# Experts: quarters of the first product of block b+1 and of the second product of block b in turn

## The reference, cut to what matters

```python
def _L0_ffn_ref(x, Wr, br, ln_g, ln_b, W1, b1, W2, b2):
    ...
    xn = (xt - mu) * jax.lax.rsqrt(var + LN_EPS)
    xe = xn[None, :, :] * ln_g[:, None, :] + ln_b[:, None, :]
    h = jax.nn.gelu(jnp.einsum('end,edh->enh', xe, W1) + b1[:, None, :], approximate=False)
    y = jnp.einsum('enh,ehd->end', h, W2) + b2[:, None, :]
    y_tok = jnp.transpose(y, (1, 0, 2))
    sel = jnp.take_along_axis(y_tok, top_idx[:, :, None], axis=1)
    out = (weights[:, :, None] * sel).sum(axis=1)
```

## Time and profile before

| | us |
|---|---|
| median of 3 timed runs | 3797.17 |
| lowest and highest of them | 3793.64, 3798.28 |
| span of the profiled execution, first to last instruction | 4365.6 |
| the experts stage in the profile | about 1370 to 2287 |

### The profile page before, as it was taken

One profiled execution on the slowest core, in us unless ns is written; L12 is line 12 of the kernel. 1 busy time (PEld: TensorE's weight loads), 2 busy tenths in 40 slices (PEclk: granted clock), 3 DMA queues, 4 the chain that ended last, 5 costly groups with the idle time before them and its releaser, 6 DMA issues. The chain is left out here.

```text
span 4365.6 us, 47498 instructions
## 1 busy us (share of the span) xinstructions
PE 3253.1 (75%) x15077; PEld 2484.5 (57%) x15077; DVE 1790.8 (41%) x5335; ACT 1496.2 (34%) x2892; POOL 2531.6 (58%) x2604
## 2 busy tenths in 40 slices
PE   1455565555446989988886798987989868999868
PEld 1344444444335777776764576655666645666547
DVE  4355565534353111111117333343333435676664
ACT  3233333323323112121115244443444434555520
POOL 6666666666643656565546666665666656666620
PEclk6677777777767999999988899988999979999978
DMA  6343334334312545554437454554544534555452
GB/s 194 111 122 109 117 115 118 116 108 120 101 40 98 176 157 179 172 185 156 157 124 269 124 146 136 149 159 116 144 138 142 166 107 143 150 153 152 135 175 103
DMA packets 396972, 609.34 MB, mean 140 GB/s; under 512 B 81648, under 2 KB 295319, under 8 KB 395943
## 3 DMA queue, kind: packets, MB, share of 16 engines
q0 software_dynamic: 115808, 279.40, 22.6%
q1 hardware_dynamic: 274182, 317.02, 22.4%
q10 hardware_dynamic: 6720, 9.74, 0.7%
HBM read 509.58 MB, written 96.33 MB: 139 GB/s over the span
## 5 line engine op out<-in xcount | busy, mean ns | idle before, releaser
L2983 POOL DMA_INDIRECT rows_h<-table,step_src x1138 | 1105.8, 972 | 688.6 <-issue 342.5
L3025 PE MATMUL bank_g<-rows_hl,counts_h 128*128 128x512 f32 x3773 | 1049.8, 422 | 89.0 <-issue 45.4
L975 POOL DMA_INDIRECT rows_r<-table,step_src x782 | 749.6, 959 | 405.2 <-issue 214.1
L3025 PEld LDWEIGHTS bank_g<-rows_hl,counts_h 128*128 128x128 f32 x3773 | 721.3, 194 | 301.9 <-issue 101.0
L1000 PE MATMUL bank_r<-rows_r,hots_r 128*128 128x257 f32 x1564 | 473.4, 457 | 457.4 <-ACT rows_r L985 227.3
L1000 PEld LDWEIGHTS bank_r<-rows_r,hots_r 128*128 128x128 f32 x1564 | 340.1, 227 | 567.6 <-ACT rows_r L985 261.6
L3184 ACT ACTIVATE counts_h<-piece_h 128x896 fp32r<-128x896 uint8 x539 | 498.1, 945 | 458.8 <-PE bank_g L3025 223.3
L1901 POOL DMA_INDIRECT kept_A<-one_d,place_d x424 | 420.7, 992 | 127.4 <-issue 127.1
L2016 PE MATMUL pY_e<-w_e,h_e 128*128 128x256 f32 x1680 | 421.7, 410 | 76.7 <-ACT h_e L1982 54.4
L1011 DVE TENSOR_SCALAR hots_r<-lane,step_dst 128x128 f32<-128x128 f32 x782 | 210.3, 289 | 593.3 <-remote 365.2
L1982 ACT ACTIVATE h_e<-pH_e,prm_e 128x256 f32<-128x256 f32 (+1 forms) x456 | 179.6, 455 | 733.7 <-PE pH_e L2005 486.5
(11 more groups left out here) (397 smaller groups left out, 3864.9 us busy)
## 6 DMA issues: line engine op xcount, KB each, us to landing
w_e<-in_L_ffn_W SPq DMA_DIRECT2D x114, 1024.0 KB
piece_h<-kept_A SPq DMA_DIRECT2D x539, 112.0 KB
kept_A<-zero_r SPq DMA_DIRECT2D x189, 112.0 KB
rows_h<-table,step_src POOLq DMA_INDIRECT x1138
table<-ACC SPq DMA_DIRECT2D x51, 256.0 KB
kept_sw<-vec_g SPq DMA_DIRECT2D x49, 256.0 KB
rows_r<-table,step_src POOLq DMA_INDIRECT x782
b_e<-in_L_ffn_b SPq DMA_DIRECT2D x57, 128.0 KB
```

Of the source, the lines that this page charges most:

```text
L975: nc.gpsimd.indirect_dma_start(out=r["rows"][:, x, 0:D], out_offset=None, in_=r["table"][:, :], in_offset=bass.IndirectOffsetOnAxis(ap=c[" ...
L2983: nc.gpsimd.indirect_dma_start(out=d["rows"][:, x, :], out_offset=None, in_=tables[l - 1][:, :], in_offset=bass.IndirectOffsetOnAxis(ap=c[ ...
L3025: mm = pe.matmul(sums, d["counts"][:, n % CV, x % PC, :], both.both(t), start=(x == 0 and i >= RINGED[l]), stop=(x == NT - 1))
```

## The change: what it does

- TensorE makes the first product of block b+1 and the second product of block b in turn, a quarter of the one and then a quarter of the other. Before the loop it makes the first product of block 0 alone. One turn of the loop over b is called a pass below.
- The turn of tokens moves: `turn(b + 2)` is now the last thing of pass b. `turn(1)` stands ahead of the loop.
- All waits for scaled inputs, weights and adds stand together at the beginning of a pass.
- `h` has two buffers, and gelu of block b waits for the second product of block b-2.
- VectorE makes the inputs of b+2 ahead of the adds of b. One semaphore, `s_xe`, now counts both the copied parameters and the scaled inputs, so that it grows by two for each block.
- The weights' loads are cut in two, `load_first` (`w1`) and `load_second` (`w2`, `b2`), each with semaphores of its own. `w1` of block b is loaded when the first product of b-3 is done, `w2` and `b2` of block b-1 when the adds of b-4 are done.
- GpSimd gathers tokens for b+3, then scatters the results of b, then issues edges. Before, it issued edges, gathered for b+2, and then scattered.
- Two semaphores of the stage ahead are used again, and counts on them start from its last value (`since`).

```diff
         @block.sync
         def _(sp):
             for b in range(WEIGHTS, NBLK):
-                sp.wait_ge(s_mm2, b - WEIGHTS + 1)
-                load_expert(sp, ins, moe, m, b, s_y)
+                sp.wait_ge(s_mm1, (b - WEIGHTS + 1) * (HJ // 2))
+                load_first(sp, ins, moe, m, b)
+                if b > WEIGHTS:
+                    sp.wait_ge(s_y, halves_before(b - WEIGHTS))
+                    load_second(sp, ins, moe, m, b - 1)
+            sp.wait_ge(s_y, halves_before(NBLK - WEIGHTS))
+            load_second(sp, ins, moe, m, NBLK - 1)
...
-                v.tensor_copy(prm[:, q, :], moe["prm"][:, bass.ds(e, 1), :].rearrange("p o n -> p (o n)")).then_inc(s_prm, 1)
-                v.wait_ge(s_prm, b + 1)
-                v.wait_ge(s_T, b + 1)
+                v.tensor_copy(prm[:, q, :], moe["prm"][:, bass.ds(e, 1), :].rearrange("p o n -> p (o n)")).then_inc(s_xe, 1)
+                v.wait_ge(s_xe, 2 * b + 1)
+                v.wait_ge(s_T, since + b + 1)
...
             inputs(0)
+            inputs(1)
             for b in range(NBLK):
-                if b + 1 < NBLK:
-                    inputs(b + 1)
+                if b + 2 < NBLK:
+                    inputs(b + 2)
                 if b > 1:
                     v.wait_ge(s_st[b % 2], 16 * halves_before(b, 2))
-                v.wait_ge(s_mm2, b + 1)
+                v.wait_ge(s_mm2, since + b + 1)
...
         def _(act):
             for b in range(NBLK):
                 w = block_of(b)[2] * P
+                if b > 1:
+                    act.wait_ge(s_mm2, since + b - 1)
                 for j in range(HJ // 2):
                     act.wait_ge(s_mm1, b * (HJ // 2) + j + 1)
...
+            def first(b, j):
+                q, halves = b % W, block_of(b)[2]
+                if b > 0:
+                    pe.wait_ge(s_h, (b - 1) * (HJ // 2) + j + 1)
+                for n in range(2):
+                    o = (2 * j + n) * P
+                    for k in range(KD):
+                        mm = pe.matmul(pH[j][:, n * BR:n * BR + halves * P], w1[:, q, k, o:o + P], xe[:, b % 2, k, 0:halves * P],
+                                       start=(k == 0), stop=(k == KD - 1))
+                mm.then_inc(s_mm1, 1)
+
+            def second(b, j):
+                q, halves = b % W, block_of(b)[2]
+                pe.wait_ge(s_h, b * (HJ // 2) + j + 1)
+                for i in (2 * j, 2 * j + 1):
+                    for m in range(halves):
+                        mm = pe.matmul(pY[m][:, 0:D], h[:, b % 2, i, m * P:(m + 1) * P], w2[:, q, i, :],
+                                       start=(i == 0), stop=(i == HJ - 1))
+                if j == HJ // 2 - 1:
+                    mm.then_inc(s_mm2, 1)
+
             turn(0)
+            pe.wait_ge(s_xe, 2)
+            pe.wait_ge(s_w1[0], 16)
+            for j in range(HJ // 2):
+                first(0, j)
+            turn(1)
             for b in range(NBLK):
-                q, halves = b % W, block_of(b)[2]
-                pe.wait_ge(s_xe, b + 1)
-                pe.wait_ge(s_w[q], 48 * (b // W + 1))
-                for j in range(HJ // 2):
...
                 if b + 1 < NBLK:
-                    turn(b + 1)
+                    pe.wait_ge(s_xe, 2 * b + 4)
+                    pe.wait_ge(s_w1[(b + 1) % W], 16 * ((b + 1) // W + 1))
+                pe.wait_ge(s_w2[b % W], 32 * (b // W + 1))
                 if b > 0:
                     pe.wait_ge(s_y, halves_before(b))
-                for j in range(HJ):
...
+                for j in range(HJ // 2):
+                    if b + 1 < NBLK:
+                        first(b + 1, j)
+                    second(b, j)
+                if b + 2 < NBLK:
+                    turn(b + 2)
...
-            for b in range(4):
+            for b in range(3):
                 tokens(b)
-                if b > 1:
-                    results(b - 2)
...
-            for b in range(2, NBLK):
-                if b + 1 < NBLK:
+            for b in range(NBLK):
+                if b + 3 < NBLK:
+                    tokens(b + 3)
+                results(b)
+                if 2 <= b < NBLK - 1:
                     for n in range(*(late * (halves_before(x) - first) // (COLS - 1 - first) for x in (b, b + 1))):
                         edges(nc, g, dram, d, EARLY[2] + n)
-                if b + 2 < NBLK:
-                    tokens(b + 2)
-                results(b)
```

More of the change, by code:

```diff
@@ L1801, in invert @@
         away = sb("away_i", [P, 3, P], F32, ctx)
-        s_c, s_v, s_hot, s_mm, s_act = sem("i_const"), sem("i_v"), sem("i_hot"), sem("i_mm"), sem("i_act")
+        s_c, s_v, s_hot, s_mm, s_act = sem("i_const"), sem("i_v"), m["s_hot"], m["s_mm"], sem("i_act")
         AWAY = [n for n in range(2 * NT) if squared(n)]
@@ L1809, in _ @@
             for b in range(WEIGHTS):
-                load_expert(sp, ins, moe, m, b)
+                load_first(sp, ins, moe, m, b)
+                load_second(sp, ins, moe, m, b)
         @block.gpsimd
@@ L1924, in experts @@
     with ExitStack() as ctx:
-        w1, w2, b2, s_w = m["w1"], m["w2"], m["b2"], m["s_w"]
+        w1, w2, b2, s_w1, s_w2 = m["w1"], m["w2"], m["b2"], m["s_w1"], m["s_w2"]
         tok = sb("tok_e", [P, 2, 2, D], F32, ctx)
@@ L1928, in experts @@
         xe = sb("xe_e", [P, 2, KD, BR], F32, ctx)
-        h = sb("h_e", [P, HJ, BR], F32, ctx)
+        h = sb("h_e", [P, 2, HJ, BR], F32, ctx)
         y = sb("y_e", [P, 2, 2, D], F32, ctx)
@@ L1935, in experts @@
         s_st = [sem(f"e_store{q}") for q in range(2)]
-        s_prm, s_T, s_xe, s_mm1, s_h, s_mm2, s_y = (sem("e_prm"), sem("e_T"), sem("e_xe"), sem("e_mm1"), sem("e_h"),
-                                                    sem("e_mm2"), sem("e_y"))
+        s_xe, s_mm1, s_h, s_y = sem("e_xe"), sem("e_mm1"), sem("e_h"), sem("e_y")
+        s_T, s_mm2, since = m["s_hot"], m["s_mm"], 2 * NT
         block = ctx.enter_context(nc.Block())
@@ L1981, in _ @@
                         k = 2 * j + n
-                        a = act.activation(h[:, k, 0:w], pH[j][:, n * BR:n * BR + w], ACT.Gelu,
+                        a = act.activation(h[:, b % 2, k, 0:w], pH[j][:, n * BR:n * BR + w], ACT.Gelu,
                                            bias=prm[:, b % 2, 2 * KD + k:2 * KD + k + 1])
@@ L1990, in turn @@
                 pe.wait_ge(s_tok[q], 16 * (halves_before(b, 2) + n))
+                if b > 0:
+                    pe.wait_ge(s_xe, 2 * b)
                 for m in range(n):
@@ L1994, in turn @@
                 mm.then_inc(s_T, 1)
-            turn(0)
-            for b in range(NBLK):
-                q, halves = b % W, block_of(b)[2]
-                pe.wait_ge(s_xe, b + 1)
-                pe.wait_ge(s_w[q], 48 * (b // W + 1))
-                for j in range(HJ // 2):
[L2002 to L2007, removed]
+            def first(b, j):
+                q, halves = b % W, block_of(b)[2]
+                if b > 0:
+                    pe.wait_ge(s_h, (b - 1) * (HJ // 2) + j + 1)
[5 more added lines that the diff above has]
+                mm.then_inc(s_mm1, 1)
@@ L2018, in _ @@
-                mm.then_inc(s_mm2, 1)
+                for j in range(HJ // 2):
[4 more added lines that the diff above has]
+                    turn(b + 2)
         @block.gpsimd
@@ L2024, in tokens @@
                 if b > 1:
-                    g.wait_ge(s_T, b - 1)
+                    g.wait_ge(s_T, since + b - 1)
                 for m in range(n):
@@ L2161, in mixture @@
         m = dict(w1=sb("w1_e", [P, WEIGHTS, KD, HID], F32, ctx), w2=sb("w2_e", [P, WEIGHTS, HJ, D], F32, ctx),
-                 b2=sb("b2_e", [P, WEIGHTS, D], F32, ctx), s_w=[sem(f"e_w{q}") for q in range(WEIGHTS)])
+                 b2=sb("b2_e", [P, WEIGHTS, D], F32, ctx), s_w1=[sem(f"e_w1{q}") for q in range(WEIGHTS)], s_w2=[sem(f"e_w2{q}") for q in range(WEIGHTS)], s_hot=sem("i_hot"), s_mm=sem("i_mm"))
         invert(nc, ins, dram, c, moe, d, m, sb, pb, sem)
@@ L2167, with expert_at, load_first, load_second @@
 WEIGHTS = 3
-def load_expert(sp, ins, moe, m, b, s_y=None):
-    q, i = b % WEIGHTS, block_of(b)[0]
-    e = sp.value_load(moe["expert"][0:1, i:i + 1], min_val=0, max_val=NE - 1)
+def expert_at(sp, moe, b):
+    i = block_of(b)[0]
+    return sp.value_load(moe["expert"][0:1, i:i + 1], min_val=0, max_val=NE - 1)
+def load_first(sp, ins, moe, m, b):
+    q, e = b % WEIGHTS, expert_at(sp, moe, b)
     w1_d = ins["L0_ffn_W1"].rearrange("e (k p) h -> p e k h", p=P)
+    sp.dma_start(m["w1"][:, q, :, :], w1_d[:, bass.ds(e, 1), :, :].rearrange("p o k h -> p (o k) h")).then_inc(m["s_w1"][q], 16)
+def load_second(sp, ins, moe, m, b):
+    q, e = b % WEIGHTS, expert_at(sp, moe, b)
     w2_d = ins["L0_ffn_W2"].rearrange("e (j p) d -> p e j d", p=P)
[L2175 to L2179, removed]
+    sp.dma_start(m["w2"][:, q, :, :], w2_d[:, bass.ds(e, 1), :, :].rearrange("p o j d -> p (o j) d")).then_inc(m["s_w2"][q], 16)
```

(1 more changed line is left out.)

## The result

| | before | changed |
|---|---|---|
| median, us | 3796.12 (4 runs, 3793.64 to 3798.28) | 3944.82 (4 runs, 3944.41 to 3945.12) |
| ratio, 95% interval | | 1.0396 [1.0381, 1.0411] |
| profiled span, us | 4365.6, and 3789.8 in a second profile (e1) | 3942.3 |

The changed kernel is 148.7 us slower; forecast were 151, with a range of 108 to 218. Its profiled span lies within 3 us of its timed runs, so this trace can be read as it stands.

A forecast was written before the change was run, and what follows sets the result against it. TensorE was taken to bound the experts stage, without waits in undisturbed blocks. Stops with start and end, 118 us, plus clock falls, 33, gave 151: from 3797 to 3948 us, range 3905 to 4015 (forecast's own 3925 to 3985).

The forecast's parts named there:

- 55 stops: Between passes, turn, VectorE's scalings and adds leave TensorE idle 1.92 us, 2.2 in all per full pass; 116 us.
- falls of the clock: TensorE's clock halves after half of the 38 full stops, 1.74 us each: 33 us, bounds 0 and 96.
- start, end, the rest of quarters in turn: Scalings of block 1 at the start, 1.4 us, and adds of block 55 at the end, about 1.1 us.
- late gathers of before, gone in the changed kernel: Token waits, 29.0 us in the first profile, taken as mostly the profile's own; gathers costed at nothing.
- The disturbed stretches: 16 stretches of the experts stage losing about 159 us to gelu and token waits, taken as mostly the profile's own.
- the other section: Skill page's "HAM oscillation" section: long idle gaps cool the clock, so these stops would cost nothing more (3915).
- the line that the profiled span would grow from 4365.6: The profiled span would grow by the same 151 us as the timed median.
- Edits costed at nothing: Gathers, cut weight loads, extra register load, doubled h, reused semaphores and parameter copy: no time on TensorE's path.
- The stop without the clock: Rival: TensorE keeps full clock through all stops, 3797 + 118 = 3915 us; chance 0.14.
- Faster: Rival: the lost 159 us are real in timed runs and the new order removes them all: 3756 us; chance 0.06.

The follow-up runs named there:

- e1: The kernel before, with no edit, profiled a second time: 3791.85 us, profiled span 3789.8 us.
- e10: Changed kernel plus 5 identity matmuls with unread results behind each turn of a pass, to keep TensorE busy: 3908.40 us, ratio 1.0302.
- e8: Changed kernel with turn in mid-pass, adds waited for behind the first quarter, and edges issued ahead of the scatter: 3786.76 us, ratio 0.9977.
- e9: Kernel before, with the gathers for b+2 issued ahead of the edges on GpSimd's queue, nothing else moved: 3777.64 us, ratio 0.9957.
- e2: Changed kernel with the turn of b+2 moved to the middle of a pass, after the second quarter: 3870.13 us, ratio 1.0195.
- e3: Changed kernel with the wait for the adds moved behind the first quarter of the first product: 3867.68 us, ratio 1.0192.
- e6: Kernel before, with only the turn of b+1 moved behind the second product of b: 3859.35 us, ratio 1.0161.
- e4: Changed kernel with the turn in the middle of a pass and the adds waited for behind the first quarter: 3830.07 us, ratio 1.0094.
- e7: Changed kernel with the edges of a pass issued ahead of the scatter of its results: 3941.19 us, ratio 1.0380.

## Why the prediction came out right, point by point

The difference of the stages taken apart by these traces (us; each stage as defined above):

| term | forecast | measured | from |
|---|---|---|---|
| 55 stops | 116 | 116.9 | stages of e10 and e8: 875.7 - 758.8 |
| falls of the clock | 33 | 37.8 | stages of changed and e10: 913.5 - 875.7 |
| start, end, the rest of quarters in turn | 2.5 | 5.4 | e8 and e9: 758.8 - 753.4 |
| late gathers of before, gone in the changed kernel | 0 | -18.6 | e9 and e1: 753.4 - 772.0 |
| gap behind the stage | 0 | 8.4 | 13.92 - 5.54 |
| sum | 151.5, stated as 151 | 149.9 | |

The medians differ by 148.7; the 1.2 us left over are less than runs of one kernel differ by. Of the 5.4 us, 2.4 are idle time (758.30 - 754.73 in e8, 752.80 - 751.64 in e9), as forecast for the start and the end; in the other 3 TensorE is busy longer, and no run parts the quarters in turn from the cut loads and the doubled `h` there.

*The stop.* Its place and size were right. Both links were shown alone (e2, e3), and the place of the turn by itself costs as much as computed in a kernel that has no quarters in turn (e6 against e9). One stop was 2.03 us and not 1.92: the scalings and adds overlap by 0.08, but from the adds' end to the matmul it took 0.26 and not 0.05.

*The clock.* I took half of the 38 full stops and none of the 17 short ones. The trace has 22 falls beside the stage's start, all behind full stops (38 of 2.02 to 2.06 us), none behind the 17 of 1.69 to 1.85. The half was a guess: of the three stops in the earlier trace rows that it went by, one had a fall. That 22 of 38 is close to it is luck, and why 16 equal stops had none is open. A pass with a fall takes 18.2 us (turn at 1216.97 to turn at 1235.17) and one without 16.5 (to 1251.72), so 1.7 each, as in the earlier trace rows. e10 shows that the cost is the clock's own: the stops were there, the falls were not. Of the two sections of the Trainium skill's page "TensorE: Matmul & The Clock Gate" that the prediction weighed, the trace agrees with "A second HAM failure mode", by which frequent micro-idles between groups of matmuls make the clock swing: 22 of the 55 stops did. It was not nearly every pass, as the prediction had read that section, and by the other section it would have been none.

*The disturbed stretches.* That they were mostly the first profile's own was right: from its first turn to its last add the stage took 913.1 us there and 772.0 in e1, so 141 us are absent. For the same reason the line that the profiled span would grow from 4365.6 failed: it is 3942.3, since the profile of the changed kernel was not disturbed. That late tokens belonged to them altogether was wrong. 13.4 us of them, with a fall of the clock, are the kernel's, and e9 removes them.

*Edits costed at nothing.* Two failed. The prediction put late gathers at nothing in both kernels; in the kernel before they cost 18.6 us (e9), and the changed kernel has none. Their lead of a block is not what removes them: e6 has the gathers' old order and none late, and e4 has the new order, with the turn in the middle of a pass and no stops, and 28.3 us of waits for tokens beyond the stage's first. And for GpSimd it looked at each pass and not at the last one, where no further pass covers the edges that now stand ahead of the last scatter: 8.4 us, 5.7 of them shown by e7. The two have opposite signs, which is why the total came nearer than its parts; that they cancel is luck.

*The rivals.* "The stop without the clock" is e10 in effect: 3908 against 3915 forecast, with the same two terms missing in the sum. "Faster" was out: with gelu and gathers a pass ahead and no stop between passes, the order of e8 gains 8 us over before, and e9 gains 17 without it.

## What to carry to other kernels

When a step moves to the end of a loop's pass, ask what the next pass waits for first: here the moved step fed it through another engine, and 2 us of latency that had been hidden stood bare 55 times. Moving a wait to the first instruction that truly needs it took 77 us of 149 away here (e3). Where an engine's queue mixes urgent transfers with filler, put the urgent ones first (17 us in e9), and look at the last pass by itself.

## What was not expected of the hardware

- A float32 matmul of the code stands in the trace as two rows and a transpose as one: 12 matmuls of 128 columns were 24 rows and 2.7 us. The counts of matmuls ahead of the prediction are such rows: the 32 of a first product are 16 matmuls of the code, a quarter's 8 are 4, and the 16 for each half of a second product are 8.
- The clock fell behind none of the 17 stops of 1.69 to 1.85 us of the changed kernel and behind 22 of its 38 of 2.02 to 2.06 us. The length of a stop alone does not tell: one of 2.82 us in e1 and two of 3.07 and 3.37 us in e4 had no fall behind them. What else decides is open.
- From the end of VectorE's adds to the matmul that waits for them it took 0.26 us (changed kernel, e2), from the end of its scalings 0.06 (e3). Why is open.
- One profile of a kernel was 576 us longer than another of the same kernel. In the longer one SyncE's register moves, 29 ns at the median, took up to 711 ns; in the other, and in the ten profiles of the changed kernel and of the other runs, 38 at most. With one such profile on record, that maximum is a sign to look for and no rule.
